# A segment attention kernel with experts on one core: the product with the probabilities made as columns, and the merge of the experts' lists by batch and in parts

## The chip, the cores and the metric

The kernel runs on one core of a Trainium2 chip. The metric is the time of one execution on the device in microseconds (us). The engines of a core are TensorE (PE, matmuls and transposes; PEld are its weight loads), VectorE (DVE), ScalarE (ACT), GpSimd (POOL) and SyncE (SP, which issues most DMA transfers).

## The reference

Two layers follow each other on x (2 batches, 2048 tokens, 256 wide), all in fp32. The first is attention over segments of 64 tokens with a memory for each of 16 heads:

```python
def step(carry, seg):                       # one segment of 64 tokens, all heads
    mem, z = carry
    qq, kk, vv = seg
    sigma_q = jax.nn.elu(qq) + 1.0
    scores = jnp.einsum('bhsk,bhtk->bhst', qq, kk) / scale      # causal mask
    att_dot = jax.nn.softmax(scores, axis=-1) @ vv
    att_mem = sigma_q @ mem / (sigma_q @ z)
    sigma_k = jax.nn.elu(kk) + 1.0
    delta = vv - sigma_k @ mem / (sigma_k @ z)
    mem_new = mem + jnp.einsum('bhsk,bhsv->bhkv', sigma_k, delta)
    z_new = z + sigma_k.sum(axis=-2, keepdims=True).transpose(0, 1, 3, 2)
    att = beta * att_mem + (1.0 - beta) * att_dot
    out = att.reshape(Bsz, SEG, H * DV) @ Wo
```

Here `out` takes the att of all 16 heads of a token in a row, reshaped from (head, token, value) without a transpose, so that 16 pieces of 4 token rows make one row of 2048. The second layer normalizes x, picks 4 of 32 experts for each token (the first 64 tokens of a batch of 256 rows that choose an expert are kept), and adds their output and that of a shared expert.

## The kernel before

The sequence is worked in 16 blocks of 128 tokens (two segments) for both batches, and each block in 4 groups of 4 heads; `n` counts the 64 groups. Each engine has its own program, written out by hand; they meet at semaphores. In a group PE does in this order: `numerators(n, g, 0)` (sigma_k and sigma_q by the memory, segment 0), the key projection of the next group (`project_t`, two halves h of two heads), `attended_transposes(n - 1)`, `update(n, 0)` (change of the memory), the query projection of the next group in two halves, of which half h waits for `k_sig` (DVE's `sigma_k(n + 1, h)`, which frees the bank), `numerators(n, g, 1)`, in group 0 `project_out`, the value projection, the transposes of the probabilities and keys, `update(n, 1)`, `attend(n)`, the product of the probabilities and the values, and the `scores` of the next group.

`attend` has 16 matmuls of fp32 per group (4 heads, 2 segments, 2 batches). Before, the probabilities `pt` of 64 tokens are stationary and the 128 value columns stream past; a matmul uses half of the rows (its batch) and half of the columns (its half), so four fit side by side:

```python
half = b if seg == 0 else 1 - b
ins = mm(seg_bank[seg][ROWS[half], j * DK:(j + 1) * DK],
         pt[ROWS[b], j, seg, :], vo[ROWS[b], seg, j, :], start=True, stop=True)
```

`seg_bank` are the two PSUM banks bank_a and bank_v. DVE's `attended(n - 1)` (L1025) then adds this product to the memory part `am`, as the first thing of the next group; PE transposes the sum with `by_piece`, which also sorts the tokens by piece; and ACT's `attended` (L767) copies it into `att`, from which `project_out` makes the output. `am` is written by ACT's `read_out` (L756), which waits for reciprocals from DVE. The memory is changed by DVE's `state_last` (head 3, L1008) and `state` (heads 0 to 2, L1015). Small steps of the norm (`x1_newton`, in group 1), of the gate (`gate_scores` in group 2, `gate_top` in group 3) and in the last block of the experts' lists (`earliest`) stand between the large ones in DVE's program.

The experts' lists: in the last block and after it, `first_earliest` finds the 64 first tokens of each expert in the first 14 blocks, in four rows of lists. `top8` (L1201, L1202) then merges: 8 rounds (`ROUNDS`) of the 8 largest and their removal over `mid`, 32 experts x 512 (four lists and the picks of block 14 for both batches), and 8 rounds over `last_picks`, 32 x 320, with the last block's picks. Between them stand `residual(NBLK)` (L1033), the norm and the gate of the last rows, on which PE's `x1_transposes(NBLK)` (L1601), the logits and the picks wait.

## Time and profile before

| what | value |
|---|---|
| median of 3 runs | 1669.26 us (1668.77 to 1669.92) |
| the profiled execution's own time | 1669.3 us |
| its span, first to last instruction | 1667.5 us, 42642 instructions |
| mean granted TensorE clock | 0.993 |
| PE busy | 1623.2 us, 97% of the span |
| PEld busy | 1418.9 us, 85% |
| DVE busy | 1143.7 us, 69% |
| ACT busy | 884.9 us, 53% |
| POOL busy | 497.9 us, 30% |
| chain that ended last | PE 93%, DVE 5%, issue 1%, ACT 1% |

Busy times of different engines overlap. A matmul's record is longer than the distance to the next one, since matmuls are pipelined; for PE the distance between starts tells what one costs. A full fp32 matmul leaves two records, a transpose or an fp32r matmul one. The times of a timeline are us from the start of the span.

### The profile page before, as it was taken

To read this page: it belongs to the slowest core of one execution; us is meant where nothing else is said; L and a number is where in the kernel's file an instruction comes from. 1 tells how busy PE (TensorE), PEld (TensorE's weight loads), DVE (VectorE), ACT (ScalarE), POOL (GpSimd) and SP (SyncE) were. 2 spreads that over 40 slices of the span, in tenths; PEclk is the share of its full clock that TensorE was granted. 3 is DMA by queue.
4 is the path that set the end of the run, shared out by engine and by line. 5 is a ranking of instruction groups with operands and counts; after the bars stand their busy time and mean duration, and the time that the engine had idled before them with its cause. 6 is when DMAs were issued, how large, how long until landed. Compare 5 with 4: busy or idle time off the path is not lost.

```text
span 1667.5 us, 42642 instructions
## 1 busy us (share of the span) xinstructions
PE 1623.2 (97%) x17190; PEld 1418.9 (85%) x17190; DVE 1143.7 (69%) x3508; ACT 884.9 (53%) x1955; POOL 497.9 (30%) x438
## 2 busy tenths in 40 slices
PE   6899999999999999999999999999999999997998
PEld 5798999899998989998999989998999989875555
DVE  6865858586775757575776758585867757688544
ACT  5664646465563646364654646464655636451131
POOL 2332323232332313231333323232323323130351
PEclk9999999999999999999999999999999999998999
DMA  5102121212202121212112021212011021228847
GB/s 183 49 21 77 35 78 33 79 30 58 58 29 85 34 71 33 86 33 68 38 44 74 29 77 36 77 33 79 31 57 58 29 88 34 73 97 263 266 90 215
DMA packets 121780, 122.06 MB, mean 73 GB/s; under 512 B 24032, under 2 KB 101296, under 8 KB 121456
## 3 DMA queue, kind: packets, MB, share of 16 engines
q1 hardware_dynamic: 118224, 113.52, 22.3%
q0 software_dynamic: 3328, 5.81, 1.8%
q8 instruction: 136, 2.23, 0.6%
q14 instruction: 60, 0.49, 0.1%
q10 hardware_dynamic: 32, 0.01, 0.0%
HBM read 94.90 MB, written 24.40 MB: 72 GB/s over the span
## 4 chain that ended last, share of the span: by engine, by line
PE 93%; DVE 5%; issue 1%; ACT 1%; DMA 0%; DVEq 0%; ACTq 0%
PE bank_p L1473 23%; PE bank_v L1591 13%; PE chain_k L1546 6%; PE chain_k L1524 6%; PE bank_a L1481 5%; PE bank_v L1481 5%; PE chain_q L1524 5%; PE bank_s L1494 4%; PE chain L1524 3%; PE bank_a L1562 3%; PE bank_p L1504 3%; PE bank_p L1648 2%; PE bank_v L1573 2%; PE bank_a L1573 2%; PE bank_s L1579 2%; PE chain L1546 2%
## 5 line engine op out<-in xcount | busy, mean ns | idle before, releaser
L588 POOL TENSOR_TENSOR step_place<-step_place 128x512 f32<-128x512 f32 x128 | 166.7, 1303 | 575.5 <-ACT step_place L734 426.5
L756 ACT ACTIVATE step_place<-chain_q,step_place 128x128 f32<-128x128 f32 x384 | 113.3, 368 | 225.3 <-DVE step_place L990 225.3
L1591 PE MATMUL bank_v<-step_place 128*128 128x256 f32 x1024 | 225.3, 381 | 0.7 <-ACT step_place L767 0.7
L1473 PE MATMUL bank_p<-xt_hi,w_hi 128*128 128x256 f32 x1024 | 220.0, 296 | 4.6 <-DVE w_lo L911 2.5
L1591 PEld LDWEIGHTS bank_v<-step_place 128*128 128x128 f32 x1024 | 193.2, 190 | 29.2 <-issue 2.6
L1473 PE MATMUL bank_p<-xt_hi,w_lo 128*128 128x256 f32 x1024 | 206.6, 283 | 0.0
L1473 PE MATMUL bank_p<-xt_lo,w_hi 128*128 128x256 f32 x1024 | 206.4, 283 | 0.0
L625 POOL TENSOR_TENSOR step_place<-step_place 128x512 f32<-128x512 f32 x64 | 69.4, 1084 | 433.2 <-DVE step_place L1251 433.2
L1473 PEld LDWEIGHTS bank_p<-xt_hi,w_hi 128*128 128x128 f32 x1024 | 158.4, 191 | 24.0 <-issue 14.5
L978 DVE SCALAR_TENSOR_TENSOR step_place<-step_place,bank_p 128x512 f32<-128x512 f32 x128 | 87.5, 684 | 109.3 <-ACT bank_p L728 109.2
L1473 PEld LDWEIGHTS bank_p<-xt_hi,w_lo 128*128 128x128 f32 x1024 | 160.0, 192 | 0.0
L1473 PEld LDWEIGHTS bank_p<-xt_lo,w_hi 128*128 128x128 f32 x1024 | 159.5, 192 | 0.0
L595 POOL TENSOR_TENSOR step_place<-step_place 128x512 f32<-128x512 f32 x128 | 150.0, 1192 | 0.0
L734 ACT ACTIVATE step_place<-bank_a 128x512 f32<-128x512 f32 x64 | 39.3, 614 | 205.7 <-PE bank_a L1481 205.7
L1033 DVE TENSOR_TENSOR rows_place<-bank_v,turned 128x512 f32<-128x512 f32 x16 | 11.1, 691 | 173.3 <-PE bank_v L1591 173.2
L1546 PE MATMUL chain_k<-step_place 64*128 64x129 f32 x762 | 118.5, 288 | 0.2 <-ACT step_place L822 0.2
L1546 PE MATMUL chain_q<-step_place 64*128 64x129 f32 x762 | 118.6, 288 | 0.0
L1546 PEld LDWEIGHTS chain_k<-step_place 64*128 64x128 f32 x762 | 94.2, 187 | 20.0 <-issue 19.3
L999 DVE SCALAR_TENSOR_TENSOR step_place<-chain_k,step_place 128x128 f32<-128x128 f32 x381 | 110.5, 346 | 0.7 <-issue 0.6
L1524 PE MATMUL chain_k<-step_place 128*64 128x129 f32 x1536 | 110.9, 279 | 0.0
L741 ACT ACTIVATE step_place<-bank_p 128x512 f32<-128x512 f32 x128 | 69.5, 596 | 75.9 <-PE bank_s L1546 75.9
L1524 PE MATMUL chain_q<-step_place 128*64 128x129 f32 x1536 | 106.4, 272 | 0.0
(219 smaller groups left out, 3959.8 us busy)
## 6 DMA issues: line engine op xcount, KB each, us to landing
step_place<-in_L_attn_Wo_dram SPq DMA_DIRECT2D x128, 256.0 KB, 2.7
step_place<-beta_all SPq DMA_DIRECT2D x64, 256.0 KB, 3.4
expert_place<-in_L_ffn_w_dram SPq DMA_DIRECT2D x24, 512.0 KB, 7.6
expert_sums<-zero SPq DMA_DIRECT2D x16, 272.0 KB, 4.9
expert_rows<-rows_place SPq DMA_DIRECT2D x15, 288.0 KB, 2.3
step_place<-in_L_attn_x_dram SPq DMA_DIRECT2D x16, 256.0 KB, 3.9
turned<-in_L_attn_x_dram SPq DMA_DIRECT2D x16, 256.0 KB, 3.9
x_rows<-rows_place SPq DMA_DIRECT2D x16, 256.0 KB, 2.8
```

The lines of the kernel that those rows point to most:

```text
L588: nc.gpsimd.tensor_tensor(dl[seg][:, :, 0:DK], val[:, seg, :, :], beta_rows[:, :, :], ALU.mult).then_inc(s["vb_ready"], 1)
L595: nc.gpsimd.tensor_tensor(vo[:, seg, :, :], val[:, seg, :, :], dl[seg][:, :, 0:DK], ALU.subtract).then_inc(s["vo_ready"], 1)
L625: nc.gpsimd.tensor_tensor(sm[:, :, :], sm[:, :, :], sinv[:, :].unsqueeze(2).to_broadcast([128, T, SEG]), ALU.mult).then_inc(s["p_ready"], 1)
L741: nc.scalar.activation(ksig[:, HB * h:HB * h + HB, :, :].rearrange("p j s d -> p (j s d)"), bank_p[h][:, :], ACT.Copy).then_inc(s["ksig_re ...
L756: ins = nc.scalar.activation(to[:, j, :], t[:, at:at + DK], ACT.Copy, scale=rd[:, seg, r:r + 1])
L978: nc.vector.scalar_tensor_tensor(out=t, in0=t, scalar=1.0, in1=bank_p[h][:, :], op0=ALU.min, op1=ALU.add).then_inc(s["k_sig"], 1)
L999: ins = nc.vector.scalar_tensor_tensor(out=dl[seg][:, j, 0:DK], in0=t[:, at:at + DK], scalar=rd[:, seg, j:j + 1], in1=dl[seg][:, j, 0:DK], ...
L1473: ins = mm(out, w[:, g, m, c, col], x[:, c, :, :].rearrange("p s t -> p (s t)"), start=i == 0, stop=i == len(parts) - 1)
L1481: ins = mm(seg_bank[seg][:, :], x[:, c, seg, :], w[:, g, 2, c, :], start=i == 0, stop=i == len(parts) - 1)
L1524: ins = mm(t[ROWS[half], at:at + ZC], sig[:, j, seg, b, :], mem[:, HG * g + j, b, :], start=True, stop=True)
L1546: ins = mm(change(b, j), ksig[ROWS[b], j, seg, :], dl[seg][ROWS[b], j, :], start=True, stop=True)
L1591: ins = mm(bank_v[:, b * D:(b + 1) * D], att[:, b * PIECES + i, :], wo[:, i % WR, :], start=(i == 0 and b == 0), stop=(i == PIECES - 1), s ...
```

## The change

In `attend` the values become the stationary operand (64 rows by 128 columns) and the 64 columns of the probabilities stream past; the result has value dimensions in its rows and tokens in its columns, bank_a for batch 0 and bank_v for batch 1. It needs no transpose any more, so the order of the rest turns round: ACT copies the product into `att` first, sorted by piece through its access pattern; PE transposes the memory part alone, and DVE adds that to `att`, later in the group than before. `numerators` puts both segments' batches in the same halves, and one `by_piece` is left. After the loop, the first merge has a row for each expert and batch (64 x 256), and its 8 rounds stand in three parts (4, 3 and 1) around the last rows' norm and gate; the second is 32 x 384.

```diff
+    MID_FIRST, MID_THEN = 4, 7
@@ placing of the lists
-    flat_toks = toks[0:E, :, :].rearrange("p e c -> p (e c)")
-    at = 4 * CAP + B * BLK
-    mid, last_picks = flat_toks[:, 0:at], flat_toks[:, at:at + CAP + B * BLK]
+    flat_toks = toks[:, :, :].rearrange("p e c -> p (e c)")
+    at = 2 * CAP + BLK
+    mid, mid_kept = flat_toks[0:B * E, 0:at], flat_toks[0:B * E, at:at + CAP]
+    at += CAP
+    last_picks = flat_toks[0:E, at:at + B * CAP + B * BLK]
@@ ACT, attended
-            for seg in range(2):
-                act.wait_ge(s["att_mm"], 2 * n + seg + 1)
-                rows = att[:, :, :].rearrange("p a (s g m) -> p a s g m", s=2, m=HG * QR)
+            act.wait_ge(s["av_mm"], n + 1)
+            for b in range(B):
+                rows = att[:, b * PIECES:(b + 1) * PIECES, :].rearrange(
+                    "p a (s g m) -> p s g m a", s=2, m=HG * QR)
                 nc.scalar.activation(
-                    rows[:, :, seg, g, :], seg_bank[seg][:, :].rearrange("p (a m) -> p a m", m=HG * QR),
-                    ACT.Copy).then_inc(s["att_ready"], 1)
+                    rows[:, :, g, :, :],
+                    seg_bank[b][:, :].rearrange("p (s m a) -> p s m a", s=2, m=HG * QR),
+                    ACT.Copy).then_inc(s["av_kept"], 1)
@@ ACT, body: attended(n - 1) moves from behind the exponential to the head of the group
@@ DVE, attended
-            dve.wait_ge(s["av_mm"], n + 1)
             for seg in range(2):
-                dve.wait_ge(s["am_ready"], 2 * n + seg + 1)
-                t = (am[0][:, n % 2] if seg == 0 else am[1][:, 0]).rearrange("p j d -> p (j d)")
-                nc.vector.tensor_tensor(t, t, seg_bank[seg][:, :], ALU.add
-                                        ).then_inc(s["att_summed"], 1)
+                dve.wait_ge(s["att_mm"], 2 * n + seg + 1)
+                t = att[:, :, :].rearrange("p a (s g m) -> p a s g m", s=2, m=HG * QR
+                                           )[:, :, seg, n % NG, :]
+                nc.vector.tensor_tensor(
+                    t, t, seg_bank[seg][:, :].rearrange("p (a m) -> p a m", m=HG * QR), ALU.add
+                    ).then_inc(s["att_ready"], 1)
@@ DVE, body
-                if n:
-                    attended(n - 1)
                 dve.wait_ge(s["s_mm"], n + 1)
...
                 if nxt:
                     sigma_k(n + 1, 0)
 
+                if n:
+                    attended(n - 1)
                 if g == 1 and not first:
                     x1_newton(blk, 2, 1)
@@ DVE, after the loop
-        for r in range(ROUNDS):
-            top8(last_picks, mid, r)
+        for r in range(MID_FIRST):
+            top8(mid_kept, mid, r)
         residual(NBLK)
...
         shared_mul(0, 1)
+        for r in range(MID_FIRST, MID_THEN):
+            top8(mid_kept, mid, r)
         gate_scores(NBLK)
...
         gate_weights(NBLK)
+        for r in range(MID_THEN, ROUNDS):
+            top8(mid_kept, mid, r)
+        for b in range(B):
+            ins = nc.vector.tensor_copy(last_picks[:, b * CAP:(b + 1) * CAP],
+                                        mid_kept[b * E:(b + 1) * E, :])
+        link(ins)
         picks(NBLK)
@@ PE, numerators
-                    half = b if seg == 0 or kind == 0 else 1 - b
-                    ins = mm(t[ROWS[half], at:at + ZC], sig[:, j, seg, b, :],
+                    ins = mm(t[ROWS[b], at:at + ZC], sig[:, j, seg, b, :],
@@ PE, attend
-                        half = b if seg == 0 else 1 - b
-                        ins = mm(seg_bank[seg][ROWS[half], j * DK:(j + 1) * DK],
-                                 pt[ROWS[b], j, seg, :], vo[ROWS[b], seg, j, :],
-                                 start=True, stop=True)
+                        c = (seg * HG + j) * SEG
+                        ins = mm(seg_bank[b][:, c:c + SEG], vo[ROWS[b], seg, j, :],
+                                 pt[ROWS[b], j, seg, :], start=True, stop=True)
@@ PE, attended_transposes
+            pe.wait_ge(s["av_kept"], 2 * n + 2)
             for seg in range(2):
-                pe.wait_ge(s["att_summed"], 2 * n + seg + 1)
+                pe.wait_ge(s["am_ready"], 2 * n + seg + 1)
```

How the change moves instructions. PE at the end of a group, from the last heads of `update` (L1546) over the product (L1562) to the scores (L1494) of the next group, before (a row with x2 is two matmuls in one row of the listing; all are fp32):

```order
2006 L1546 MATMUL chain<-step_place 128x129
2007 L1546 MATMUL bank_s<-step_place 128x129
2008 L1562 MATMUL bank_a<-step_place 64x128 x2
2009 L1562 MATMUL bank_v<-step_place 64x128 x2
2010 L1562 MATMUL bank_a<-step_place 64x128 x2
2011 L1562 MATMUL bank_v<-step_place 64x128 x2
2012 L1562 MATMUL bank_a<-step_place 64x128 x2
2013 L1562 MATMUL bank_v<-step_place 64x128 x2
2014 L1562 MATMUL bank_a<-step_place 64x128 x2
2015 L1562 MATMUL bank_v<-step_place 64x128 x2
2016 L1494 MATMUL bank_s<-step_place 64x64 x16
```

The same place of the changed kernel (`update` is L1563 there, the product L1580, the scores L1513), where the product has the rows 2240 to 2255; its end:

```order
2251 L1580 MATMUL bank_v<-step_place 128x64
2252 L1580 MATMUL bank_a<-step_place 128x64
2253 L1580 MATMUL bank_v<-step_place 128x64
2254 L1580 MATMUL bank_a<-step_place 128x64
2255 L1580 MATMUL bank_v<-step_place 128x64
2256 L1513 MATMUL bank_s<-step_place 64x64 x16
```

There are 16 matmuls in both, but each now fills 128 output rows, and the banks change with each one.

DVE in the middle of a group 2, before: the first and the second half of `sigma_k` (L978), the gate's scores between them (L1055 to L1057) and head 3 of the state (L1008):

```order
L978 SCALAR_TENSOR_TENSOR step_place<-step_place,bank_p 128x512
L1055 TENSOR_SCALAR eg<-eg 128x64
L1056 RECIPROCAL rows_place<-eg 128x64
L1057 TENSOR_TENSOR rows_place<-rows_place,gbias 128x64
L1008 TENSOR_TENSOR step_place<-step_place,chain 128x129
L1008 TENSOR_TENSOR step_place<-step_place,bank_s 128x129
L978 SCALAR_TENSOR_TENSOR step_place<-step_place,bank_p 128x512
```

The same place of the changed kernel (L983 is `sigma_k`, L1061 to L1063 the gate's scores, L1013 the state):

```order
L983 SCALAR_TENSOR_TENSOR step_place<-step_place,bank_p 128x512
L1030 TENSOR_TENSOR step_place<-step_place,bank_a 128x32x16
L1030 TENSOR_TENSOR step_place<-step_place,bank_v 128x32x16
L1061 TENSOR_SCALAR eg<-eg 128x64
L1062 RECIPROCAL rows_place<-eg 128x64
L1063 TENSOR_TENSOR rows_place<-rows_place,gbias 128x64
L1013 TENSOR_TENSOR step_place<-step_place,chain 128x129
L1013 TENSOR_TENSOR step_place<-step_place,bank_s 128x129
L983 SCALAR_TENSOR_TENSOR step_place<-step_place,bank_p 128x512
```

The two adds, which stood ahead of the mask, now stand between the two halves of `sigma_k`.

## Rows read from the trace of the kernel before

**Rows 1.** Stages of the run: us, busy of each engine, PE clock, DMA

```profile
200.00:1480.00 1280.00, 1279.88 (x14356) 1155.65 (x14353) 891.11 (x2803) 722.07 (x1600) 382.70 (x330) 1.00 0.19 56
```

**Rows 2.** PE timeline, end of a group 1: start us, us, what

```profile
814.84 0.27 PE L1546 MATMUL chain_k<-step_place 64*128 64x129 f32 x1
...
815.07 0.27 PE L1546 MATMUL chain<-step_place 64*128 64x129 f32 x1
...
815.43 0.28 PE L1562 MATMUL bank_a<-step_place 64*64 64x128 f32 x2
...
816.09 0.28 PE L1562 MATMUL bank_a<-step_place 64*64 64x128 f32 x2
...
816.30 1.15 PE L1494 MATMUL bank_s<-step_place 128*64 128x64 f32 x32
817.29 0.83 PE L1524 MATMUL chain_k<-step_place 128*64 128x129 f32 x12
```

**Rows 3.** PE weight loads in the timeline, the logits of the same group

```profile
813.16 0.97 PEld L1609 LDWEIGHTS bank_a<-gwt,turned 128*128 128x128 f32 x8
```

**Rows 4.** DVE timeline, the group 2 that follows

```profile
816.73 0.68 DVE L1025 TENSOR_TENSOR step_place<-step_place,bank_a 128x512 f32<-128x512 f32 x1
817.32 0.68 DVE L1025 TENSOR_TENSOR step_place<-step_place,bank_v 128x512 f32<-128x512 f32 x1
...
822.53 0.69 DVE L978 SCALAR_TENSOR_TENSOR step_place<-step_place,bank_p 128x512 f32<-128x512 f32 x1 [1.90 <-ACT bank_p L728]
823.14 0.19 DVE L1055 TENSOR_SCALAR eg<-eg 128x64 f32<-128x64 f32 x1
...
824.32 0.29 DVE L1008 TENSOR_TENSOR step_place<-step_place,chain 128x129 f32<-128x129 f32 x1
...
824.72 0.68 DVE L978 SCALAR_TENSOR_TENSOR step_place<-step_place,bank_p 128x512 f32<-128x512 f32 x1
```

**Rows 5.** DVE timeline, the same place in a group 1 and a group 3

```profile
802.20 0.69 DVE L978 SCALAR_TENSOR_TENSOR step_place<-step_place,bank_p 128x512 f32<-128x512 f32 x1 [1.51 <-ACT bank_p L728]
...
803.19 0.16 DVE L940 SCALAR_TENSOR_TENSOR rs_x<-b_x,rs_x 128x2 f32<-128x2 f32 x1
...
842.22 0.69 DVE L978 SCALAR_TENSOR_TENSOR step_place<-step_place,bank_p 128x512 f32<-128x512 f32 x1 [1.53 <-ACT bank_p L728]
...
843.14 0.17 DVE L1095 COPY tlist<-ttop 128x8 f32<-128x8 f32 x1
```

**Rows 6.** PE timeline, start of query projection half 1 in groups 1, 2, 3

```profile
805.24 0.40 PE L1473 MATMUL bank_p<-xt_hi,w_hi 128*128 128x256 f32 x2
...
825.73 0.40 PE L1473 MATMUL bank_p<-xt_hi,w_hi 128*128 128x256 f32 x2
...
845.41 0.40 PE L1473 MATMUL bank_p<-xt_hi,w_hi 128*128 128x256 f32 x2
```

**Rows 7.** ACT timeline, group 2: read-out and a copy into att

```profile
819.58 0.89 ACT L756 ACTIVATE step_place<-chain_q,step_place 128x128 f32<-128x128 f32 x3 [3.05 <-DVE step_place L990]
...
824.87 0.64 ACT L767 ACTIVATE step_place<-bank_v 128x512 f32<-128x512 f32 x1
```

**Rows 8.** Timeline after the loop, first PE, then DVE

```profile
1501.76 14.08 PE L1591 MATMUL bank_v<-step_place 128*128 128x256 f32 x64 [0.69 <-ACT step_place L767]
...
1527.94 1.12 PE L1601 MATMUL bank_v<-ident,rows_place 128*128 128x128 f32 x4 [8.67 <-DVE rows_place L946]
...
1531.47 3.75 PE L1667 MATMUL bank_s<-shared_place 128*128 128x256 f32 x8
...
1547.20 1.89 PE L1667 MATMUL bank_s<-shared_place 128*128 128x256 f32 x8
...
1510.95 0.67 DVE L1201 MAX8 shared_place<-shared_place 32x8 f32<-32x512 f32 x1
...
1522.88 0.69 DVE L1033 TENSOR_TENSOR rows_place<-bank_v,turned 128x512 f32<-128x512 f32 x1
...
1549.05 0.48 DVE L1201 MAX8 shared_place<-shared_place 32x8 f32<-32x320 f32 x1
```

More of the change, by code:

```diff
@@ L205, in layer @@
     ident = sb("ident", [128, 128])
-    by_piece = [take([128, 128]) for i in range(2)]
+    by_piece = take([128, 128])
     turned = sb("turned", [128, NC * B * BLK])
@@ L555, in _ @@
         nc.gpsimd.memset(ident[:, :], 0.0).then_inc(s["ident_ready"], 1)
-        for i in range(2):
-            nc.gpsimd.memset(by_piece[i][:, :], 0.0).then_inc(s["ident_ready"], 1)
-        pool.wait_ge(s["ident_ready"], 3)
+        nc.gpsimd.memset(by_piece[:, :], 0.0).then_inc(s["ident_ready"], 1)
+        pool.wait_ge(s["ident_ready"], 2)
         nc.gpsimd.affine_select(out=ident[:, :], in_=ident[:, :], compare_op=ALU.not_equal,
@@ L561, in _ @@
                                 ).then_inc(s["ident_ready"], 1)
-        for i in range(2):
-            nc.gpsimd.affine_select(out=by_piece[i][:, :], in_=by_piece[i][:, :],
-                                    compare_op=ALU.not_equal, fill=1.0, base=-SEG * i,
-                                    pattern=[[-SEG + 2 * SEG * i, 2], [-1, PIECES], [-PIECES, QR]],
-                                    channel_multiplier=1).then_inc(s["ident_ready"], 1)
+        nc.gpsimd.affine_select(out=by_piece[:, :], in_=by_piece[:, :],
+                                compare_op=ALU.not_equal, fill=1.0, base=0,
+                                pattern=[[-SEG, 2], [-1, PIECES], [-PIECES, QR]],
+                                channel_multiplier=1).then_inc(s["ident_ready"], 1)
         nc.gpsimd.memset(mask[:, :], 0.0).then_inc(s["const_ready"], 1)
@@ L793, in body @@
                 nxt = not (last and g == NG - 1)
+                if n:
+                    attended(n - 1, (g - 1) % NG, None if first or g == 0 else blk)
                 read_out(n, 0)
```

25 lines of the change are left out of this document (14 added, 11 removed).

## The prediction

> **What bounds the kernel now.** I read the page first, where TensorE (PE) is far ahead of all others, and then the stages: from 200 to 1480 us PE is busy 1279.88 of 1280.00 us at full clock [rows 1], and the view of waits has no PE entry at all in that stretch. So in the 14 middle blocks each microsecond added to PE's own list, or to the last thing that PE waits for, is a microsecond of the run; what VectorE (DVE), ScalarE (ACT) and GpSimd do costs nothing until PE waits for it. Then I read PE's timeline around the product with the probabilities for the distance between starts, since that is what a pipelined instruction costs [rows 2], and DVE's timeline around the place where the change puts its adds [rows 4]. Last I read the stretch after the loop, where PE does wait, 8.67 us at one place [rows 8].
>
> **Part 1, the product (PE).** A full fp32 matmul is two records in the trace. Before, the 16 matmuls of a group are 32 records on four 64x64 tiles: two records for bank_a and two for bank_v start together, and the next four 0.11 us later (815.43 to 816.09 is six steps in 0.66 us) [rows 2]. So eight steps of 0.11 us. From the last step of the state update (815.07) to the first of the scores (816.30) is 1.23 us; in it is a change of tile shape on each side, which costs more than a step (816.09 to 816.30 is 0.21 us, not 0.11).
>
> After, the same 16 matmuls have a stationary of 64 rows by 128 columns (the values) and stream 64 columns (the probabilities). Each fills all 128 array columns, so only two can lie side by side, one per half of the rows: 16 pairs of records instead of eight fours. No row of before has this shape, so the pair's step is bounded. The update has the same 64x128 stationary, in pairs, with 129 streamed columns: one pair per 0.11 us (814.84 to 815.07 is two of them) [rows 2]. The question is whether the step is set by 129 streamed columns or by the 128 stationary ones. The logits answer it: 128 stationary columns and only 32 streamed, and still 8 loads in 0.97 us of 0.19 us each, so (0.97-0.19)/7 = 0.11 us per step [rows 3]. Loading 128 columns sets 0.11 us however little is streamed. The low end is the scores, 64 stationary and 64 streamed: 16 pairs in 816.30 to 817.29, 0.062 us [rows 2]. The high end is two row halves that do not overlap, 0.22 us per pair. I take 0.11, since both rows with 128 stationary columns have it. Update and product now have one shape, so the change between them goes: 0.11 + 15 x 0.11 + 0.20 = 1.96 us against 1.23, +0.73 us per group. 63 groups (the last is in part 3): **+46 us**. At 0.062 it would be -2 us, at 0.22 +157 us.
>
> The Trainium skill bears on this twice. TensorE: Matmul & The Clock Gate, section LDWEIGHTS (loading the stationary operand), gives the load's time as its columns over 1.2 GHz: 107 ns for 128, 53 for 64. By that rule the sum is the one above, and the trace agrees (0.11 us at 32 streamed columns). TensorEngine Tiling, section When to Use Tiling, advises to swap the operands and tile the columns where the streamed dimension is at most 64; by this rule the layout of before is the good one and the change goes the wrong way.
>
> **Part 2, the two adds move inside the group (DVE).** Before, DVE adds the memory part to the product right after the scores (L1025, 0.60 us from start to start), before it masks [rows 4]. Nothing on PE was near: taking them away lets mask and maximum come sooner, but the reciprocal that releases ACT's read-out needs PE's numerators and the key activations need the key projection, so it gains next to nothing. Now the order is: ACT copies the product out first, PE transposes the memory part, and DVE adds after sigma_k of half 0 (L978) and before the rest. ACT's two copies (0.64 us each, even doubled by the new stride) fit in the 3.05 us that it idles before the read-out [rows 7]; the transposes stay 8, at their place. Neither makes PE wait.
>
> The adds are not covered. They now stand in the short piece between the first L978, which waits for ACT, and the second, for which PE waits before the query projection of half 1. Group 2: first L978 at 822.53, then 0.61, adds 1.19, the gate's three operations 1.18 (823.14 to 824.32), the state's last head 0.40, so the second starts at 825.91 instead of 824.72 and is done at about 826.64 (0.68 and a semaphore). PE wants it at 825.73: **0.91 us of new wait** [rows 4, 6]. Group 1: 802.20+0.61+1.19+0.55+0.40+0.73 = 805.68 against 805.24: 0.44. Group 3: 842.22+0.61+1.19+0.52+0.40+0.73 = 845.67 against 845.41: 0.26. The 0.55 and 0.52 are the small operations that stand there in each [rows 5, 6]. Group 0 has none such: as group 2 without the 1.18, 825.46 against 825.73, no wait. That is 1.61 us per block, 22.5 us for 14 blocks; in the last block operations of the experts' lists stand there too in groups 0 and 1, and I put twice a block on it, 3.3 us (an estimate). Sum **+26 us**. Queued behind the second L978 are the state of three heads (PE's next numerators) and the denominators; PE has the whole of half 1 to do first, so I see no second wait. Bounds: 0 if the first L978 can start 1 us earlier; twice the price of an add (its SBUF side now has runs of 16 elements) would add 1.2 us in three groups and 0.9 in the fourth, +64 us. The nearest operation on the same runs is ACT's copy into att, 0.64 us against 0.68 for an add [rows 4, 7], so I take the plain price.
>
> **Part 3, after the loop.** Before, DVE does all 8 rounds of the merge (1510.95 to 1522.88, 1.49 us each at 512 wide) ahead of the residual, though the output projection (1501.76 and 14.08 us) is done at 1515.8; PE then waits 8.67 us for the normed rows and runs on at half clock: 8 records take 3.75 us where the same 8 take 1.89 later [rows 8]. Now 4 rounds stand ahead and they are 256 wide. An operation of a round takes 0.67 us at 512 and 0.48 at 320 [rows 8], 1 ns per element, and a round is two of them and 0.15: 0.98 us at 256 and 1.24 at 384. What is late first: the last product is 0.8 us longer, and the adds now wait for copy, copy and transposes, so they start about 2.5 us later and the lists behind them too; the output projection starts 1.1 us later and ends at 1517.0. Residual at about 1517.3 instead of 1522.9, PE's transposes 5.6 us sooner, and with 2 us of waiting instead of 8.7 most of the slow clock (about 3 us) goes: 8.6 us. Given back: shared_down(1) before at 1547.20 would now come at 1538.6, but the DVE product it needs stands behind the gate, round 8, two copies and three rounds of 1.24: done at 1540.7. That leaves **-6.5 us** at the token step. The expert phase behind it is a chain of the same pieces, moved as a whole. Bounds: -9 (nothing given back) and +3 (nothing gained but the later start, since the weight loads also start 2.5 us later and may hold up the first gathers).
>
> **Sum.** 46 + 26 - 6.5 = +65.5 us on the profiled execution's own 1669.3 us (span 1667.5 and 1.8 around it), which is also the median of the runs: **1735 us**.
>
> **Rivals.**
> *No new waits*: the adds find cover, because ACT is freed earlier and the first L978 with it. For it: DVE idles 1.5 to 1.9 us before that instruction; against: it waits there for ACT, which waits for the key projection. 1669.3+46-6.5 = 1709 us.
> *The load is hidden*: the pair's step goes to that of the scores, 0.062 us. For it: the scores pay for what they stream; against: their stationary is 64 wide and the logits show 0.11 at 128. -2+26-6.5: 1687 us.
> *Faster, the product pays by streamed columns*: each record costs half of now (0.0275/2 us), so a pair takes 0.0275. Then 16 x 0.0275+0.20 = 0.64 us against 1.23, -37 us, and -37+26-6.5 gives 1652 us. It decides below 0.045 us per pair, where 63 x (16 s - 1.03) + 19.5 is zero. For it: in the product of before a record costs 0.0275; against: that takes four tiles at a time, and no row with 128 stationary columns goes under 0.11 per step.
> *Dearer*: row halves one after the other, or adds at twice the price: 1799 to 1846 us. Against: the update's pairs overlap to 0.01 us.
>
> **How the numbers follow.** Forecast 0.70, no new waits 0.14, load hidden 0.06, faster 0.05, dearer 0.05. The range 1703 to 1757 takes in the forecast with its terms off (waits 10 to 45 us, product 41 to 50, tail -9 to +3) and the no-wait case; outside are the other three and a little of the spread. 0.2% (3.3 us) is about what a measurement of this kernel can tell from no change: faster 0.05, same 0.01, slower 0.94.
>
> **What would show it.** In the changed profile: the product's records as pairs 0.11 us apart and 1.96 us from the last update pair to the scores; a wait of PE on sigma_k's second half, about 0.9, 0.45, 0.25 and 0 us in groups 2, 1, 3 and 0; the adds at 0.6 us; PE's wait for the last normed rows about 2 us instead of 8.7, and no half clock behind it. The prediction is wrong if pairs start 0.06 us apart, if PE's waits are elsewhere, or if the expert phase begins no sooner after the loop.

## The result, and the profile of the changed kernel

The changed kernel takes 1738.97 us (median of 4 runs, 1738.22 to 1740.07); the kernel before took 1669.01 us beside it (4 runs, 1668.22 to 1669.92). The ratio is 1.0419, 95% interval 1.0404 to 1.0435: slower by 70 us, where 66 were predicted. The profiled execution has a span of 1736.4 us.

The time is best divided at the first matmul of the `scores`, which PE makes once per group. From scores to scores, in us (read in one block from the starts of the first records on PE's timeline, good to 0.01; the other blocks from 1 to 14 agree to 0.04, but for one group 3 of the changed kernel, which took 20.88):

| | group 0 | group 1 | group 2 | group 3 | block |
|---|---|---|---|---|---|
| before | 33.06 | 20.48 | 19.68 | 19.38 | 92.60 |
| changed | 33.79 | 21.63 | 21.38 | 20.53 | 97.33 |
| difference | 0.73 | 1.15 | 1.70 | 1.15 | 4.73 |

Up to the first scores (27.21 us before, 26.77 now) nothing has changed much; from the first to the 64th scores (1485.07 and 1557.94) the kernel lost 73.3 us; behind them it won 3.9 (182.42 and 178.51 us to the end of the span).

**The product.** PE's timeline of the changed kernel at the end of a group 1, which answers [rows 2] (start us, length us, engine and line, what):

```profile
948.52 0.27 PE L1563 MATMUL chain<-step_place 64*128 64x129 f32 x1
948.63 0.22 PE L1580 MATMUL bank_a<-step_place 64*128 64x64 f32 x1
948.63 0.22 PE L1580 MATMUL bank_v<-step_place 64*128 64x64 f32 x1
948.68 0.27 PE L1580 MATMUL bank_a<-step_place 64*128 64x64 f32 x1
...
948.80 0.27 PE L1580 MATMUL bank_a<-step_place 64*128 64x64 f32 x1
...
950.25 0.27 PE L1580 MATMUL bank_a<-step_place 64*128 64x64 f32 x1
...
950.46 1.15 PE L1513 MATMUL bank_s<-step_place 128*64 128x64 f32 x32
```

Records come in pairs, one for each bank, 0.11 us apart (only the first pair is followed after 0.05), and it is 1.94 us from the last step of the update to the scores (1.96 were predicted, 1.23 it was before). Group 0, where nothing else was added, is 0.73 us longer.

**The adds.** DVE's timeline in the group 2 behind it answers [rows 4]:

```profile
956.65 0.69 DVE L983 SCALAR_TENSOR_TENSOR step_place<-step_place,bank_p 128x512 f32<-128x512 f32 x1 [1.99 <-ACT bank_p L730]
957.26 0.68 DVE L1030 TENSOR_TENSOR step_place<-step_place,bank_a 128x512 f32<-128x512 f32 x1
957.86 0.68 DVE L1030 TENSOR_TENSOR step_place<-step_place,bank_v 128x512 f32<-128x512 f32 x1
958.45 0.19 DVE L1061 TENSOR_SCALAR eg<-eg 128x64 f32<-128x64 f32 x1
...
959.63 0.29 DVE L1013 TENSOR_TENSOR step_place<-step_place,chain 128x129 f32<-128x129 f32 x1
...
960.04 0.68 DVE L983 SCALAR_TENSOR_TENSOR step_place<-step_place,bank_p 128x512 f32<-128x512 f32 x1
```

The second half of `sigma_k` starts 3.39 us behind the first (3.38 predicted); an add costs its 0.60 us from start to start, though it writes in runs of 16 elements. PE's timeline has the wait that follows, here for groups 1 and 2:

```profile
938.61 0.51 PE L1492 MATMUL bank_p<-xt_hi,w_hi 128*128 128x256 f32 x2 [0.21 <-DVE step_place L983]
...
960.78 0.51 PE L1492 MATMUL bank_p<-xt_hi,w_hi 128*128 128x256 f32 x2 [0.73 <-DVE step_place L983]
```

Such a wait is counted from the modelled end of the matmul ahead, which lies some 0.2 us behind the start of what could have followed. So it shows 0.21 and 0.73 where the groups grew by 0.42 and 0.97 beyond the product's 0.73. The view of waits adds them up; there was no PE entry for this line in the middle of the run before:

```profile
PE bank_p L1492 <- DVE step_place L983: 20.4, 47, 1.5
```

**The tail.** PE's timeline behind the last scores answers [rows 8] (in brackets how long PE was idle, and for whom it waited):

```profile
1574.53 1.12 PE L1591 MATMUL bank_a<-step_place 128*128 128x128 f32 x4 [1.98 <-ACT step_place L771]
...
1577.28 15.62 PE L1609 MATMUL bank_v<-step_place 128*128 128x256 f32 x64 [0.78 <-DVE step_place L1030]
1598.07 0.66 PE L1619 MATMUL bank_v<-ident,rows_place 128*128 128x128 f32 x4 [1.73 <-DVE rows_place L951]
...
1600.33 3.20 PE L1685 MATMUL bank_s<-shared_place 128*128 128x256 f32 x8
```

And DVE's timeline at the residual:

```profile
1593.00 0.69 DVE L1039 TENSOR_TENSOR rows_place<-bank_v,turned 128x512 f32<-128x512 f32 x1 [1.35 <-PE bank_v L1609]
```

PE's wait for the normed rows is 1.73 us instead of 8.67, as predicted. But the output projection starts 19.34 us behind the last scores instead of 16.69, and takes 15.62 us instead of 14.08. The stages of the changed kernel (columns: length, busy time of PE, PEld, DVE, ACT and POOL, then the granted PE clock) say why:

```profile
1570.00:1574.00 4.00, 2.00 (x32) 1.89 (x32) 1.57 (x4) 1.86 (x3) 0.00 (x0) 0.95 0.21 74
1574.00:1582.00 8.00, 6.69 (x23) 5.48 (x24) 6.01 (x9) 0.99 (x3) 0.00 (x0) 0.60 0.01 2
1582.00:1590.00 8.00, 8.00 (x39) 7.04 (x38) 7.65 (x18) 0.00 (x0) 0.00 (x0) 1.00 0.60 170
```

PE was busy half of the time up to 1574; then the clock falls to its lower level of 1.2 GHz for most of 8 us, in the transposes (1.12 us, where they take 0.60 in the loop) and in the first part of the projection. ACT's two copies (L771), for which PE waits here, have a group of the view by lines each:

```profile
L771 ACT ACTIVATE step_place<-bank_v 128x512 f32<-128x512 f32 x64 | 73.6, 1151 | 0.0
L771 ACT ACTIVATE step_place<-bank_a 128x512 f32<-128x512 f32 x64 | 70.7, 1105 | 42.1 <-PE bank_v L1580 42.1
```

1.13 us for one copy, where I had put the old 0.64 [rows 7] and called the doubled time harmless for the loop.

### The profile page after: what moved, and what is told of

It reads as the page before. It is cut to its first block, busy times and chain, and to the rows that moved or that the text cites. A ratio compares the mean times of both kernels' runs of the same rounds, so it can differ in the third digit from the quotient of the medians.

```text
span 1736.4 us, 42641 instructions
## 1 busy us (share of the span) xinstructions
PE 1680.3 (97%) x17190; PEld 1480.9 (85%) x17190; DVE 1148.7 (66%) x3509; ACT 962.2 (55%) x1955; POOL 499.1 (29%) x436
## 4 chain that ended last, share of the span: by engine, by line
PE 75%; DVE 17%; ACT 6%; issue 2%; DMA 0%; DVEq 0%; ACTq 0%
PE bank_v L1609 13%; PE bank_p L1492 11%; PE bank_a L1580 6%; PE chain_k L1541 5%; PE bank_a L1500 5%; PE bank_v L1500 5%; PE chain_q L1541 5%; PE bank_s L1513 4%; PE chain_k L1563 4%; DVE step_place L983 3%; DVE step_place L1030 3%; PE chain L1541 3%; DVE step_place L1004 3%; PE bank_p L1523 3%; ACT step_place L727 2%
## 5 line engine op out<-in xcount | busy, mean ns | idle before, releaser
L1492 PE MATMUL bank_p<-xt_hi,w_hi 128*128 128x256 f32 x1024 | 224.8, 301 | 24.2 <-DVE step_place L983 20.4
L627 POOL TENSOR_TENSOR step_place<-step_place 128x512 f32<-128x512 f32 x64 | 69.3, 1083 | 498.2 <-DVE step_place L1260 498.2
L983 DVE SCALAR_TENSOR_TENSOR step_place<-step_place,bank_p 128x512 f32<-128x512 f32 x128 | 87.5, 685 | 114.5 <-ACT bank_p L730 114.5
L720 ACT ACTIVATE step_place<-bank_p 128x512 f32<-128x512 f32 x128 | 76.6, 599 | 113.7 <-PE bank_p L1492 113.7
L1580 PE MATMUL bank_a<-step_place 64*128 64x64 f32 x1024 | 121.2, 269 | 1.2 <-DVE shared_place L1129 1.2
L1580 PE MATMUL bank_v<-step_place 64*128 64x64 f32 x1024 | 121.2, 269 | 0.0
L1580 PEld LDWEIGHTS bank_a<-step_place 64*128 64x128 f32 x1024 | 119.1, 188 | 1.5 <-DVE shared_place L1129 1.5
L1580 PEld LDWEIGHTS bank_v<-step_place 64*128 64x128 f32 x1024 | 119.1, 188 | 0.0
L1563 PE MATMUL chain_q<-step_place 64*128 64x129 f32 x762 | 118.6, 288 | 0.0
L1563 PE MATMUL chain_k<-step_place 64*128 64x129 f32 x762 | 118.5, 288 | 0.0
```

Source lines behind the costliest of these rows:

```text
L720: nc.scalar.activation(part(qraw, h), bank_p[h][:, :], ACT.Copy).then_inc(s["q_raw"], 1)
L983: nc.vector.scalar_tensor_tensor(out=t, in0=t, scalar=1.0, in1=bank_p[h][:, :], op0=ALU.min, op1=ALU.add).then_inc(s["k_sig"], 1)
L1492: ins = mm(out, w[:, g, m, c, col], x[:, c, :, :].rearrange("p s t -> p (s t)"), start=i == 0, stop=i == len(parts) - 1)
L1563: ins = mm(change(b, j), ksig[ROWS[b], j, seg, :], dl[seg][ROWS[b], j, :], start=True, stop=True)
L1580: ins = mm(seg_bank[b][:, c:c + SEG], vo[ROWS[b], seg, j, :], pt[ROWS[b], j, seg, :], start=True, stop=True)
```

## The experiments

**The merge alone.** The kernel before with the new merge of the lists (by batch, 4 + 3 + 1 rounds) and nothing else:

```diff
-        for r in range(ROUNDS):
-            top8(last_picks, mid, r)
+        for r in range(MID_FIRST):
+            top8(mid_kept, mid, r)
         residual(NBLK)
...
+        for r in range(MID_FIRST, MID_THEN):
+            top8(mid_kept, mid, r)
         gate_scores(NBLK)
...
+        for r in range(MID_THEN, ROUNDS):
+            top8(mid_kept, mid, r)
...
```

> The kernel before with only the merge of the lists changed (by batch, 64 x 256, rounds in parts of 4, 3 and 1; last merge 32 x 384). My theory: the changed kernel's tail is late by its longer chain from the last product to the output projection (ACT's two copies at 1.1 us, a half clock start), so the merge alone gains more than the 3.6 us seen there: the residual can start right after the output projection, 7 us sooner, and most of the half clock goes: 7 to 9 us faster than before, about 1661 us. Rival, the gain is eaten by the DMA engines, which are full until the expert weights have arrived: under 4 us, 1665 us or more.

1662.48 us (1662.27 to 1663.22); ratio 0.9956, 0.9942 to 0.9970. The groups are those of before (92.60 per block). This half of the change is worth 7.3 us and beats both kernels (6.7 us of it lie behind the last scores in the two profiled executions, 175.75 us against 182.42). PE's timeline of this kernel:

```profile
1501.96 14.08 PE L1608 MATMUL bank_v<-step_place 128*128 128x256 f32 x64 [0.69 <-ACT step_place L771]
1521.20 0.66 PE L1618 MATMUL bank_v<-ident,rows_place 128*128 128x128 f32 x4 [1.73 <-DVE rows_place L950]
...
1524.27 3.76 PE L1684 MATMUL bank_s<-shared_place 128*128 128x256 f32 x8
```

The projection keeps its 14.08 us, and the wait falls to 1.73. But the 8 records of shared_down still take 3.76 us, as the 3.75 of before [rows 8]: the slow clock behind the wait, which I had counted as saved, stays. Here it costs something: PE's transposes of the picks come behind these records, and DVE idles 1.07 us ahead of the masked picks (L1133, shown with the last run).

**The loop alone.** The changed kernel with the old merge:

```diff
-        for r in range(MID_FIRST):
-            top8(mid_kept, mid, r)
+        for r in range(ROUNDS):
+            top8(last_picks, mid, r)
         residual(NBLK)
...
```

> The changed kernel with the old merge. My theory: the whole loop cost stays (73 us) and the tail is no longer shortened: 1739 + 5 to 9 us, about 1745 us. Rival, the merge did nothing in this kernel and the tail's 3.6 us came from elsewhere (for instance longer overlap of the weight loads with the slower loop): 1739 us.

1747.78 us (1745.61 to 1748.27); ratio 1.0463, 1.0447 to 1.0479; groups as in the changed kernel (97.30 per block). So the new product with its adds costs 78.0 us over the kernel before that ran beside it (1669.83 us). The changed kernel is 8.8 us shorter, 8.0 if each is taken against the kernel before beside it: that the merge gives back. Part of it is the clock, for without the new merge the output projection takes longer still:

```profile
1576.20 17.08 PE L1594 MATMUL bank_v<-step_place 128*128 128x256 f32 x64 [0.78 <-DVE step_place L1028]
```

17.08 us instead of the changed kernel's 15.62, behind the same waits (1.31, 1.99 and 0.78 us, there 1.21, 1.98 and 0.78).

**64 stationary columns.** Only the first 64 value columns are loaded, and 64 output rows made; half of the product is left out:

```diff
-                        ins = mm(seg_bank[b][:, c:c + SEG], vo[ROWS[b], seg, j, :],
+                        ins = mm(seg_bank[b][0:SEG, c:c + SEG], vo[ROWS[b], seg, j, 0:SEG],
```

> The changed kernel with only 64 of the 128 value columns as the stationary operand of the product; it leaves out half of the product (the other half of each bank keeps old numbers). Same count of matmuls, same 64 streamed columns, same pairs. My theory: the load of 128 columns paces a pair at 0.11 us; with 64 it falls to the scores' 0.06 us, the product's stretch from 1.96 to about 1.25 us (one change of tile shape comes back), 64 x 0.7 = 45 us: about 1694 us, a little more if the shorter product exposes other work. Rival, a pair costs 0.11 us whatever it loads (streaming or a fixed cost): 1739 us.

1698.20 us (1696.19 to 1700.12); ratio 1.0175, 1.0158 to 1.0192. All four groups are 0.66 us shorter than in the changed kernel (33.13, 20.96, 20.71, 19.87), 64 x 0.66 = 42 us, with 40.8 measured (45 expected). PE's timeline, from the third and fourth pair of a product to the scores:

```profile
904.08 0.22 PE L1580 MATMUL bank_a<-step_place 64*64 64x64 f32 x1
...
904.14 0.22 PE L1580 MATMUL bank_a<-step_place 64*64 64x64 f32 x1
...
905.00 1.15 PE L1513 MATMUL bank_s<-step_place 128*64 128x64 f32 x32
```

0.06 us per pair with half of the stationary columns and the same 64 streamed.

**128 streamed columns.** The other way round: all 128 stationary columns and twice the streamed ones (both segments' results are written to one place, so part of the result is lost):

```diff
-                        c = (seg * HG + j) * SEG
...
-                                 pt[ROWS[b], j, seg, :], start=True, stop=True)
+                        c = j * BLK
...
+                                 pt[ROWS[b], j, :, :].rearrange("p s q -> p (s q)"),
+                                 start=True, stop=True)
```

> The changed kernel with 128 streamed columns in the product (both segments' probabilities) instead of 64; the extra columns are overwritten or wrong, so part of the product is lost. My theory: the load sets the pace and hides twice the stream: no change, 1739 us within 3 us, pairs still 0.11 us apart. Rival, the streamed columns are paid: a pair takes 0.16 us or more, +50 us or more, 1790 us.

1739.19 us (1738.29 to 1741.90); ratio 1.0420, 1.0403 to 1.0438: the changed kernel's time. Each group is 0.05 us longer (group 1 took 21.68 us, with 21.63 in the changed kernel), since here the first pair too is followed after 0.11 us and not 0.05. Its pairs in such a group, the second and the third of a product:

```profile
927.38 0.27 PE L1580 MATMUL bank_a<-step_place 64*128 64x128 f32 x1
...
927.49 0.27 PE L1580 MATMUL bank_a<-step_place 64*128 64x128 f32 x1
```

The two runs together settle the product: its step is what the 128 stationary columns cost, 0.11 us, and the 64 streamed ones, even doubled, hide in it but for 0.05 us per group. That agrees with the rule for LDWEIGHTS in the Trainium skill, TensorE: Matmul & The Clock Gate, which the prediction weighed (107 ns for 128 columns and 53 for 64, here 0.11 and 0.06 us).

**Both batches in one half of the rows.** Do the pair's two loads run side by side because they go to different halves of the rows? Here both batches take their operands from rows 0 to 63 (batch 1 gets batch 0's values):

```diff
-                        ins = mm(seg_bank[b][:, c:c + SEG], vo[ROWS[b], seg, j, :],
-                                 pt[ROWS[b], j, seg, :], start=True, stop=True)
+                        ins = mm(seg_bank[b][:, c:c + SEG], vo[ROWS[0], seg, j, :],
+                                 pt[ROWS[0], j, seg, :], start=True, stop=True)
```

> The changed kernel with both batches' matmuls of the product in the first half of the rows, so that batch 1 gets batch 0's product (wrong for it). My theory: the two row halves did overlap, and now cannot: 32 records 0.11 us apart instead of 16 pairs, +1.76 us per group, +113 us: about 1850 us. Rival, the halves took turns all along: no change, 1739 us.

1929.03 us in a single run, 190 us over the changed kernel and 79 over what was expected. The product's records (two to a line now) and the start of the scores, then two stages whose last figures but two are the clock:

```profile
925.13 0.38 PE L1580 MATMUL bank_v<-step_place 64*128 64x64 f32 x2
925.35 0.38 PE L1580 MATMUL bank_a<-step_place 64*128 64x64 f32 x2
...
928.12 1.48 PE L1513 MATMUL bank_s<-step_place 128*64 128x64 f32 x32
```

```profile
920.00:940.00 20.00, 19.80 (x198) 18.38 (x196) 11.86 (x38) 10.21 (x20) 5.92 (x5) 0.91 0.20 54
940.00:960.00 20.00, 20.00 (x211) 18.76 (x210) 12.54 (x38) 10.97 (x24) 7.04 (x6) 0.91 0.14 41
```

Two records take 0.22 us, one 0.11: nothing overlaps. From 924.51 to the scores the product takes 3.61 us instead of 1.83, the 1.78 us more that the step gives, 64 x 1.78 = 114 us. That much was expected. The groups grew by more, 2.98 us each on average (from the first to the last scores 1719.1 us against 1531.2). The rest, some 76 us, goes with the clock: it was granted at 1.00 in the same stages of the changed kernel and at 0.91 here. In the trace of this run it falls to its lower level about three times in a block, in 35 of 48 cases within 1.2 us behind the start of a product's last matmul, for example behind this one:

```profile
924.50:928.10 3.60, 3.60 (x36) 3.55 (x32) 1.42 (x4) 1.08 (x2) 1.26 (x1) 1.00 0.20 44
928.80:932.20 3.40, 3.40 (x46) 3.40 (x42) 1.62 (x4) 1.77 (x2) 2.85 (x3) 0.50 0.03 11
```

From the first to the last scores it was at this level for 174 us, which can cost at most 87 us. PE had no idle time before this fall (3.60 of 3.60 us busy); why the clock falls with this product, no run tells.

**The adds behind the state.** DVE's two adds go behind the second half of `sigma_k` and the state, so that PE's query projection doesn't wait:

```diff
-                if n:
-                    attended(n - 1)
...
                 state(n, g, 0)
+                if n:
+                    attended(n - 1)
```

> The changed kernel with DVE's two adds moved from between the halves of sigma_k to behind the state of heads 0 to 2; nothing else. My theory: PE's waits before half 1 of the query projection (0.42, 0.96 and 0.42 us in groups 1, 2, 3) were due to those adds and go, and nothing waits at the new place: 14 x 1.8 = 25 us and some 3 us of the first and last block, 1739 to about 1711 us, each group 0.73 us longer than before. Rival, DVE is short of time in the whole group and the wait only moves to the probability transposes or the read-out: 1725 us or more.

1728.32 us (1726.69 to 1730.15); ratio 1.0346, 1.0330 to 1.0362. Of the 28 us expected, 10.7 came: my theory that the adds have cover there fell. The waits show what stands in their place (us in total, times, longest):

```profile
PE bank_v L1619 <- DVE rows_place L951: 11.9, 16, 1.7
...
PE bank_p L1492 <- DVE step_place L983: 1.6, 2, 1.3
```

The waits for `sigma_k` are gone, as meant. Over before and the product's 0.73 the groups now lose 0, 0.68, 0 and 0.27 us instead of 0, 0.42, 0.97 and 0.42. In group 1 PE's `x1_transposes` wait for `x1_apply`, which stands behind the adds. In group 3 the product waits for `pickv_ready`, the masked picks, the last link of the gate's operations on DVE. DVE's timeline there and then PE's:

```profile
982.72 0.39 DVE L1120 TENSOR_SCALAR rows_place<-wsel,wsum 128x32 f32<-128x32 f32 x2
983.14 0.28 DVE L1140 TENSOR_TENSOR rows_place<-bank_a,desc 64x128 f32<-64x128 f32 x1
```

```profile
983.18 0.27 PE L1563 MATMUL bank_s<-step_place 64*128 64x129 f32 x1
983.47 0.32 PE L1580 MATMUL bank_a<-step_place 64*128 64x64 f32 x1
```

The product starts right behind the end of L1140 (983.42), 0.29 us behind the last step of the update instead of 0.11. That is 0.95 us per block instead of 1.81, 12 us for 14 blocks. And the tail gave some back, 183.8 us in the profiled execution instead of 178.5. The stages of this kernel ahead of its output projection:

```profile
1554.00:1558.00 4.00, 1.85 (x27) 1.40 (x22) 3.69 (x18) 1.63 (x5) 1.04 (x1) 1.00 0.00 0
1558.00:1570.00 12.00, 9.24 (x49) 7.94 (x50) 6.04 (x11) 2.40 (x4) 0.00 (x0) 0.50 0.07 25
```

A new wait of 0.94 us ahead of the last probability transposes, for POOL (L627), comes beside the old one of 1.21 us ahead of the last product. PE is busy 1.85 of 4 us, and from 1558 on the clock is at half for more than 12 us, the last product included. The profiled execution is the longest of the four (1730.15 us, the shortest 1726.69), so this part of the loss differs from one execution to the next.

**The adds by group.** As the last, but in group 1 the adds stay between the halves of `sigma_k` (the edit is shown against the last run):

```diff
                 if g == 1 and not first:
+                    attended(n - 1)
                     x1_newton(blk, 2, 1)
...
                 state(n, g, 0)
-                if n:
+                if n and (g != 1 or first):
                     attended(n - 1)
```

> The kernel with the adds behind the state, in which one group goes back: in group 1 the two adds stand where the changed kernel has them, between the two halves of sigma_k, in groups 0, 2 and 3 behind the state. Theory: the late adds pushed x1_apply in group 1, for whose rows PE waited some 0.67 us at x1_transposes; in the middle of the group they cost 0.42 us (the wait for sigma_k's second half). So group 1 takes 21.63 us again instead of 21.87, PE's 14 waits at x1_transposes go and those for sigma_k in group 1 come back, and the time falls by 14 x 0.25 = 3.5 us from 1728.3: 1725. Rival: the wait at x1_transposes has another cause (the longer product ahead of group 1); then it stays, the wait for sigma_k is added to it, and the time is 1734.

1724.66 us (1721.43 to 1726.12); ratio 1.0335, 1.0319 to 1.0350. Group 1 takes 21.62 us again, the others 33.78, 20.39 and 20.38: 3.7 us, with 3.5 expected. The stages ahead of its output projection are those of the last run, with the same waits for POOL and DVE, but here the clock fell only behind the last product:

```profile
1550.00:1554.00 4.00, 1.85 (x26) 1.40 (x23) 3.69 (x19) 1.63 (x5) 1.04 (x1) 1.00 0.00 0
1554.00:1558.00 4.00, 2.02 (x33) 1.89 (x33) 0.90 (x1) 2.12 (x4) 0.00 (x0) 0.84 0.21 74
1558.00:1562.00 4.00, 3.22 (x11) 2.56 (x11) 2.83 (x5) 0.28 (x1) 0.00 (x0) 0.50 0.00 0
```

The tail takes 179.3 us instead of 183.8. This profiled execution is the shortest of its four (1721.43 us).

**The adds behind x1_apply.** In group 1 they go further back still (again against the adds behind the state):

```diff
                 state(n, g, 0)
-                if n:
+                if n and (g != 1 or first):
                     attended(n - 1)
...
                 if g == 1 and not first:
                     x1_apply(blk)
+                    attended(n - 1)
```

> The kernel with the adds behind the state, in which in group 1 the two adds stand still later: behind x1_apply, whose rows PE transposes, and ahead of delta(n, 1). Theory: the adds stood ahead of the thing PE waits for, and nothing else is late. Then x1_apply is done 1.2 us sooner, PE's wait of 0.67 us at x1_transposes goes, and the adds are done at about 13.4 us from the start of the scores, where PE wants the bank they read for the value projection at about 13.3 to 13.6: the wait left is 0 to 0.3 us. Group 1 takes 21.2 to 21.5 us instead of 21.87, and the time is 1728.3 minus 5 to 9: 1719 to 1723. Rival: the bank is wanted by the value projection before the adds have read it, and PE waits there for what it waited for before: 1728, no gain.

1727.70 us (1725.14 to 1727.89); ratio 1.0345, 1.0329 to 1.0361: the rival was right, though PE waits for the bank at the transposes, ahead of the value projection. PE's timeline in that group:

```profile
934.81 0.66 PE L1620 MATMUL bank_v<-ident,rows_place 128*128 128x128 f32 x4 [0.58 <-DVE step_place L1030]
```

The same transposes wait, now for the bank: they write into bank_v, which the second add has still to read (group 1: 21.83 us, against 21.88 with the adds ahead of `x1_apply`). So in group 1 the adds are boxed in on both sides, 0.42 us is the least of the three places tried, and the adds cost the loop something wherever I put them.

**The copy in runs.** ACT's copy wrote each element 512 bytes behind the last; here its loop is turned round, so that it writes runs of 16 elements (64 bytes) and reads the bank with a step of 64 bytes:

```diff
-                rows = att[...].rearrange("p a (s g m) -> p s g m a", s=2, m=HG * QR)
+                rows = att[...].rearrange("p a (s g m) -> p s g a m", s=2, m=HG * QR)
...
-                    seg_bank[b][:, :].rearrange("p (s m a) -> p s m a", s=2, m=HG * QR),
+                    seg_bank[b][:, :].rearrange("p (s m a) -> p s a m", s=2, m=HG * QR),
```

> The changed kernel with ACT's copy of the product walking the other way round, so that it writes runs of 16 elements into att and reads the bank with a stride, instead of writing each element 512 bytes from the last; same values. My theory: the copy goes from 1.13 us to 0.6 and nothing in the loop notices (it is covered by 3 us of idle), after the loop the chain to the output projection is 1 us shorter and perhaps starts at full clock (1.5 us): 1739 to about 1737 us. Rival, the strided read of the bank costs as much: 1739 us and copies of 1.1 us. Second rival, the copies do hold the loop (POOL and PE wait for the bank): 10 us or more faster.

1738.15 us (1738.03 to 1740.18); ratio 1.0412, 1.0396 to 1.0428. The two groups of ACT's copies in this kernel:

```profile
L771 ACT ACTIVATE step_place<-bank_a 128x512 f32<-128x512 f32 x64 | 38.2, 597 | 42.1 <-PE bank_v L1580 42.1
L771 ACT ACTIVATE step_place<-bank_v 128x512 f32<-128x512 f32 x64 | 37.9, 592 | 0.0
```

Half of the price goes, 68 us of ACT's time in all, and the kernel has the same time within what can be measured: in the loop ACT's copies are covered, and in the tail PE's transposes still wait 1.18 us for them instead of 1.98, and then run at half clock. The output projection starts 0.80 us sooner behind the last scores (18.54 instead of 19.34) but takes 16.08 us instead of 15.62, so that 0.34 us are left at its end. The same turned copy with the adds behind the state (copy edit and adds edit together):

> The changed kernel with both mends, the adds behind the state and the copy in runs of 16. My theory: the gains add, since one is in the loop and the other after it: about 1709 us. Rival, the longer copy was hidden behind the adds' wait and shows once that is gone, or the reverse: 4 us or more off the sum of the two.

1725.05 us (1723.48 to 1726.27); ratio 1.0330, 1.0313 to 1.0347: 3.3 us less than the late adds alone, with the same groups (96.43 us per block). It is in the tail, 180.1 us in the profiled execution instead of 183.8. The 1709 us expected were built on the 1711 expected of the late adds, and missed with them by 16; that the gains add held within the spread: 10.7 and 0.8 us one by one, 13.9 together.

**Five, three and no rounds.** The merge alone, its rounds divided otherwise: DVE idles 1.16 us ahead of the residual, and a round takes 0.98:

```diff
-    MID_FIRST, MID_THEN = 4, 7
+    MID_FIRST, MID_THEN = 5, 8
```

> The old loop with the new merge, its 8 rounds divided as 5 ahead of the residual and 3 ahead of the gate, none behind the gate, instead of 4, 3 and 1. In the run with 4, DVE idles 1.16 us ahead of the residual for PE, and a round takes 0.98 us: the fifth is free there. Behind the gate one round of 0.98 us goes, which stood ahead of the picks and of the DVE product for which shared_down(1) waits 1.4 us. Theory: DVE's list after the loop is what the token step waits for, so the time falls by up to 1 us, from 1662.5 to 1661.5. Rival: the fifth round is done after PE's output projection by a little, or the token step waits for PE: no change, 1662.5.

1662.51 us (1662.45 to 1664.64); ratio 0.9965, 0.9952 to 0.9979: no change, the rival was right in the number. The fifth round was free, for DVE still idles ahead of the residual:

```profile
1515.50 0.69 DVE L1037 TENSOR_TENSOR rows_place<-bank_v,turned 128x512 f32<-128x512 f32 x1 [0.19 <-PE bank_v L1608]
```

It starts 30.65 us behind the last scores, as in the merge alone. PE's wait for the normed rows is 2.05 us instead of 1.73 all the same, since the two small operations L928 of the norm take 0.31 us longer here (0.20 of it idle between them), for which the profile gives no cause. The round taken from behind the gate gains nothing, since the masked picks (L1133) start only when PE's transpose of the picks has ended. The idle time ahead of them grew instead, in the merge alone and in this kernel:

```profile
1533.99 0.57 DVE L1133 TENSOR_TENSOR shared_place<-bank_a,desc 32x128 f32<-32x128 f32 x2 [1.07 <-issue]
```

```profile
1533.40 0.57 DVE L1133 TENSOR_TENSOR shared_place<-bank_a,desc 32x128 f32<-32x128 f32 x2 [1.67 <-issue]
```

## Why the prediction was right

**What bounds the kernel.** Right: each microsecond added to PE's list or to its waits came through. 4.73 us per block times 14 is 66 of the 70 us. (The range was to take in the terms at their bounds, but the upper ones add up to 1669.3 + 50 + 45 + 3 = 1767 us, above its 1757.)

**Part 1, the product.** Right, in size and cause: 1.94 us instead of 1.96, and 0.73 us in group 0. 63 x 0.73 = 46 us as predicted. Against the rival of the hidden load stands the run with 128 streamed columns, and against both faster rivals the 0.06 us that appear only once 64 stationary columns are left; for the step of 0.11 with the halves side by side stands the run with one half, where it doubles.

**Part 2, the adds.** Right in place and size: 0.42, 0.97, 0.42 and 0 us in groups 1, 2, 3 and 0, against 0.44, 0.91, 0.26 and 0. That makes 1.81 us per block instead of 1.61, 25.3 us in place of 22.5. The miss in group 3 is mostly in the small operations between the adds and the state (979.83 to 980.46 us in the changed kernel): 0.63 us, where the prediction took 0.52. First scores to last grew by 73.3 us against a predicted 72, so about 2 us are left for the first and the last block (3.3 predicted). The plain price of an add held. The rival of no new waits fell with the waits themselves, and that the adds cause them is shown by the run with the adds behind the state, where the waits for `sigma_k` go; the later place covers the adds in groups 0 and 2 only.

**Part 3, the tail.** Right in sign, and its term mis-sized: -3.9 us, not -6.5. The step that failed is "the output projection starts 1.1 us later and ends at 1517.0". It starts 2.65 us later and takes 1.54 us longer, 4.2 us instead of 1.1. ACT's copies, for which I had 0.64 us [rows 7], last 1.03 and 1.06 there: with the copies in runs the start comes 0.80 us sooner. The rest goes largely with the clock, which falls to half behind PE's waits: each four transposes take 1.12 and 1.06 us, before 0.66, and the projection's first part is slow. The residual still comes sooner with respect to the last scores, 35.06 us instead of 37.81, but 2.75 sooner and not 5.6. All behind it went as the prediction had it: PE waits for DVE's list at `shared_down(1)`, which starts 58.4 us behind the last scores; by the prediction's 1540.7 it was 55.6, and these 2.8 us, the residual's, are the miss of the term. "No half clock behind it" failed too, 3.20 us for the 8 records in the changed kernel and 3.76 in the merge alone; in the changed kernel it cost nothing, since DVE's list was later (PE still waits 0.23 us for it). In the merge alone, where the projection is as before, the transposes start 7.15 us sooner (35.72 us behind the last scores, 42.87 before), and that brought most of the 7.3 us. On top of the new loop the merge is worth 8.0 to 8.8 us; the 0.7 to 1.5 us more than in the merge alone are about what the longer half clock in the loop alone costs (its projection takes 17.08 us, that of the changed kernel 15.62). Whether the merge or chance shortened it is not shown.

**The sum.** The misses did not cancel: +2.8 us in the waits, -1.3 in the first and last block, +2.6 in the tail and -0.4 ahead of the first scores turn 65.5 into 69.2, and the profiled executions differ by 68.9. The number is right because its largest term, the product's 46 us, is.

**The experiments' own misses.** The adds behind the state were to win 28 us. That sum had the waits of all groups at nothing, and overlooked that `x1_apply` and the picks stand behind the adds on DVE, with PE waiting for both. It also took the tail as fixed. The run with one row half was to take 1850 us and took 1929: the product grew as expected, the fall of the clock was not foreseen. For the adds behind `x1_apply` theory and rival had the value projection want the bank which the second add reads; it was the transposes ahead of it.

## What to carry to other kernels

Price a swap of the stationary and the streamed operand by the step between starts in rows of the same stationary width: here the 128 stationary columns set it, with 64 streamed columns as with 128. On the engine that releases the bound one, an operation is free only at a place where nothing behind it is waited for within its time: list every such consumer in every phase of the loop before moving it, the banks included. And split a change of several parts: here one half was worth 7.3 us, and the other hid it.

## What the runs showed that I had not expected

- ACT's copy of 128x512 fp32 out of PSUM takes 1.13 us when each element is written 512 bytes behind the last, and 0.60 us when it writes runs of 64 bytes; that it then reads the bank with a step of 64 bytes costs nothing (before, with the same runs and a read without a step, it took 0.63 us). The Trainium skill's page SBUF — State Buffer (The DMA port swizzle) speaks of lines of 16 bytes, with a penalty for each access that crosses to a new one; the two copies here agree with that for a write.
- Two matmuls of 64 rows on the same half of the rows do not overlap at all (0.22 us for a pair of records, 0.11 on different halves), and PE's clock fell to 0.91 in stages of 20 us where it was 1.00 in the changed kernel, with PE busy 19.80 of 20 us and no idle time in the 3.60 us ahead of one fall. This is a single run.
- The same idle stretch of PE (1.85 of 4 us busy) was followed by half clock at once in one execution (the adds behind the state) and some 3 us later in another (the adds by group), and the tail took 183.8 and 179.3 us. The times of such kernels spread more, 1726.7 to 1730.2 and 1721.4 to 1726.1 us, than those of the changed kernel, 1738.2 to 1740.1.
